# Attention in one transformer layer: two key tiles of values and the due sum in one visit to the 32-column matmuls, sums inverted in transposed blocks

## The chip, the core and the metric

The program runs on one core of a Trainium2 chip. A core has a matrix engine (TensorE; PE in the profile, its weight loads PEld), three elementwise engines (VectorE, DVE; ScalarE, ACT; GpSimd, POOL), and SyncE (SP), which here only issues DMAs. They run at the same time and wait for each other by semaphores. TensorE writes to PSUM, eight banks of 2 KB in each of 128 partitions; POOL does not touch PSUM in this program. The metric is the device time of one execution, in microseconds (us); lower is better.

## The reference

A layer with block-sparse causal self attention, cross attention and a feed-forward block, in 32-bit floats, for B = 4 batch rows, S = 1024 tokens, D = 512 channels, 16 heads of 32 channels. Cut to what matters here:

```python
x = _layernorm(tgt, n1_g, n1_b)
tgt = tgt + _block_sparse_self_attn(x, ...)
x = _layernorm(tgt, n2_g, n2_b)
tgt = tgt + _mha_cross(x, memory, ...)
x = _layernorm(tgt, n3_g, n3_b)
return tgt + jax.nn.relu(x @ ff_w1.T + ff_b1) @ ff_w2.T + ff_b2

# inside each attention
scores = jnp.einsum('bhqd,bhkd->bhqk', q, k) / scale   # self: masked by block and causally
p = jax.nn.softmax(scores, axis=-1)
out = jnp.einsum('bhqk,bhkd->bhqd', p, v)
```

## The kernel before

The layer is a row of stages: projections of the context (tag d_) and of x (a_), self attention (b_), a projection (c_), cross attention (e_), a projection (f_), the feed-forward block (m_). The change touches `attention_stage` alone, which is built twice, with `causal` true for b_ and false for e_.

**A pass.** Four heads of one batch row are worked on together; 4 rows by 4 such head groups make N = 16 passes, numbered n. The 1024 queries are two halves of 512. A pass is a list of steps k, each one tile of 128 keys (t) against one half (h) of queries: 16 steps in cross attention, all 512 queries wide; 12 in self attention, where a tile on the diagonal leaves only the later queries, 384, 256 or 128 columns, and tiles beyond it are left out. `first` is the first query column that a step needs. Each step has four blocks, one for each head j.

**What a step does, and on which engine.**
- TensorE, `scores`: keys by queries into one of two PSUM buffers `st_ps` (tile st). The stationary operand is 128 wide; it also holds rows with the negative row maximum, so that the exponential needs no bias. On the diagonal of self attention a short mask matmul follows (line 1136).
- ScalarE, `exponentials`: exp of a block into `probs`, a ring of PR key tiles (6 in self attention, 8 in cross).
- TensorE, `weigh`: the probabilities against the values of the tile. The stationary operand is 32 columns wide, and the four heads fill four strips of 32 output rows of `pv_ps`. Operands are 32-bit; the profile counts each such matmul twice.
- POOL (line 974): adds the probabilities of the two or three key tiles of a group (`groups`), head by head, in place, onto the first tile of the group.
- TensorE, `sum_up`: a 32-column matrix of ones against the added tile, into `sum_ps`. This gives the softmax sum of each query, the same number on each of the 32 rows of a head. The columns of one group are cut into `parts` (2 or 3), one part at the end of each step.
- ScalarE, `copy_sums` (line 1071): `sum_ps` to `sums`, once each half. VectorE, `copy_outs` (line 988): `pv_ps` to `outs`, once each half.
- VectorE, `normalise`: in pieces of 64 columns (cross) or 128 (self), one piece a step, reciprocal of `sums` and product with `outs`.
- In the same steps TensorE and VectorE prepare the row maxima of the next passes: `max_scores` (tile nat; one or two matmuls for each of 32 units of 128 queries and one head, a unit being t and j) and `maximum` (line 997). In cross attention units alternate between two pairs of PSUM banks, and unit u may be written once unit u-2 is reduced (`reach` is 2; in self attention 2 to 4). Once a pass the 32 columns of maxima are transposed (line 1120) and split in a high and a low part (lines 1006, 1008).

**What sets the order.** Nothing schedules: the loops of `body` on each engine are the order. On TensorE, step k goes over j = 0 to 3 and issues for each j: scores of block (k+1, j); the row-maximum matmuls that the tables `next_units` and `later_units` put there (in cross attention one unit at j = 0 and one at j = 2); after j = 1 `weigh(k)`; after j = 3 the parts of sums due at step k. So values and sums alternate, each between two scores:

```python
if j == 1:
    weigh(n, p, k)
if j == HG - 1:
    for back, g, c in summing[k]:
        if at_least(n, back):
            sum_up(n - back, p - back, g, c)
```

VectorE goes over the same steps and j: copy of outputs at j = 2 of a half's last step, split of maxima, maxima, and at j = 2 the due piece of `normalise`. Passes 1 to 12 run in a loop of three passes an iteration; the others are written out.

**Waits that matter.** `scores` of a block waits for the exponential of two blocks before (`exped`). `sum_up` of a half's first group waits until `sum_ps` is free (`sums_copied`). The exponential into a ring buffer waits for the sum of the tile that lay there (`summed`). The addition of a group waits for the values of its first tile (`weighed`), since it overwrites it.

## Time and profile before

| what | us |
|---|---|
| median of 3 runs | 3573.18 (3571.24 to 3574.4) |
| span of the profiled execution, first to last instruction | 3571.7 |
| self attention, b_ | about 601 to 1349 of the span |
| cross attention, e_ | about 1652 to 2659 |
| feed-forward block, m_ | about 2760 to the end |

The profiled execution's own time was not taken apart from its span, which lies 1.5 us below the median.

How to read the rows below. A row of the view in order of time has the start in us, the time in us, the engine, the line in the kernel, the operation, written and read tiles with their shapes, and the count of like instructions merged in the row. Matmuls are pipelined, so the start of the next row tells more than the time in a row: "start to start" is what an instruction costs its engine. In brackets stands how long the engine (or its weight loader) had been idle before, and what ended the wait. A row of the view by tile has least, median and greatest time of one instruction in ns. e_sum matmuls are the sums, e_pv the values, e_st the scores, e_nat the row maxima.

### The profile page before, as it was taken

The numbers are of one execution on the slowest core, as the hardware profiler recorded it, in microseconds if no ns is written. First come the engines' busy times: TensorE is split into PE (matmuls) and PEld (weight loads), VectorE is DVE, ScalarE is ACT, GpSimd is POOL, SyncE is SP. The second block draws the span as 40 slices with busy tenths as digits, with TensorE's granted clock in tenths as the row PEclk, the third lists the DMA queues.
The fourth block names the chain that finished last, engine by engine and source line by source line (L and its number), as shares of the span: only waits on it lengthen the run. The fifth ranks groups of instructions, "written<-read, shape, count | busy, mean of one in ns | idle before, by whom it ended". The sixth has DMA issues, their size and how long they took to land. (4 is left out here: it accounts for less than half of the span.)

```text
span 3571.7 us, 54829 instructions
## 1 busy us (share of the span) xinstructions
PE 3303.2 (92%) x18570; PEld 2078.1 (58%) x18570; DVE 2124.1 (59%) x2949; ACT 1323.5 (37%) x2369; POOL 1826.2 (51%) x1552
## 2 busy tenths in 40 slices
PE   7969997999999996969999999999968499999999
PEld 6857884545454545754444444444427388888887
DVE  4435545777777765757998989899948611111110
ACT  2112221545455552223665656566642221111111
POOL 3124332444444455644887878788876362222222
PEclk9979996999999998987999999999989799999999
DMA  5535446343444405534332423324026631111110
GB/s 195 177 118 195 170 162 152 83 89 79 88 96 96 96 14 179 214 131 104 73 69 52 93 49 72 74 52 93 10 77 233 250 95 48 51 49 51 50 48 24
DMA packets 211665, 361.36 MB, mean 101 GB/s; under 512 B 16312, under 2 KB 92600, under 8 KB 207312
## 3 DMA queue, kind: packets, MB, share of 16 engines
q1 hardware_dynamic: 211408, 358.01, 35.2%
q8 instruction: 152, 2.49, 0.3%
q14 instruction: 105, 0.86, 0.1%
HBM read 214.20 MB, written 142.61 MB: 100 GB/s over the span
## 5 line engine op out<-in xcount | busy, mean ns | idle before, releaser
L974 POOL TENSOR_TENSOR e_probs<-e_probs 128x512 f32<-128x512 f32 x640 | 799.2, 1280 | 234.6 <-ACT e_probs L1064 228.8
L1064 ACT ACTIVATE e_probs<-e_st 128x512 f32<-128x512 f32 x1024 | 603.4, 597 | 428.5 <-PE e_st L1132 369.6
L997 DVE TENSOR_REDUCE e_neg_max<-e_nat 128x1 f32<-128x1024 f32 x512 | 615.1, 1214 | 92.9 <-PE e_nat L1110 67.1
L974 POOL TENSOR_TENSOR b_probs<-b_probs 128x128 f32<-128x128 f32 (+2 forms) x384 | 341.7, 920 | 427.7 <-ACT b_probs L1064 427.7
L1064 ACT ACTIVATE b_probs<-b_st 128x512 f32<-128x512 f32 (+3 forms) x768 | 367.2, 491 | 419.1 <-PE b_st L1136 331.2
L997 DVE TENSOR_REDUCE b_neg_max<-b_nat 128x1 f32<-128x128 f32 (+7 forms) x512 | 369.5, 751 | 184.0 <-PE b_nat L1114 180.1
L1132 PE MATMUL e_st<-e_qs,e_ks 99*128 99x512 f32 x1024 | 464.0, 459 | 10.4 <-issue 7.6
L1363 DVE CAST m_hid_hi<-m_hid 128x512 fp32r<-128x512 f32 x128 | 59.1, 462 | 599.1 <-ACT m_hid L1315 599.1
L1342 POOL TENSOR_TENSOR m_hid_lo<-m_hid,m_hid_hi 128x512 fp32r<-128x512 f32 x128 | 165.1, 1290 | 461.5 <-DVE m_hid_hi L1363 461.5
L1132 PEld LDWEIGHTS e_st<-e_qs,e_ks 99*128 99x128 f32 x1024 | 192.9, 190 | 339.4 <-ACT e_probs L1064 233.2
L1110 PE MATMUL e_nat<-e_ks,e_qs 96*128 96x512 f32 x1024 | 351.6, 429 | 27.0 <-DVE e_neg_max L997 15.5
L1132 PE MATMUL b_st<-b_qs,b_ks 99*128 99x512 f32 (+2 forms) x768 | 332.2, 447 | 10.0 <-issue 9.0
L1315 ACT ACTIVATE m_hid<-m_h_ps,m_b 128x512 f32<-128x512 f32 x128 | 88.2, 689 | 589.8 <-PE m_h_ps L117 589.8
L1147 PE MATMUL e_pv<-e_probs,e_vs 128*32 128x512 f32 x2048 | 278.0, 615 | 0.5 <-ACT e_probs L1064 0.5
L1110 PE MATMUL b_nat<-b_ks,b_qs 97*128 97x384 f32 (+4 forms) x768 | 249.3, 410 | 26.3 <-DMA b_ks<-b_key_mask 19.3
L1132 PEld LDWEIGHTS b_st<-b_qs,b_ks 99*128 99x128 f32 x768 | 150.6, 196 | 202.2 <-ACT b_probs L1064 149.8
L1110 PEld LDWEIGHTS e_nat<-e_ks,e_qs 96*128 96x128 f32 x1024 | 199.5, 202 | 81.1 <-DVE e_neg_max L997 42.5
L117 PE MATMUL m_h_ps<-m_x_hi,m_w_hi 128*128 128x512 f32 x512 | 201.4, 393 | 24.0 <-DMA m_x_lo<-xt_lo 21.7
L117 PE MATMUL m_o_ps<-m_w_hi,m_hid_hi 128*128 128x512 f32 x512 | 202.6, 396 | 0.6 <-POOL m_hid_lo L1342 0.6
L117 PE MATMUL m_o_ps<-m_w_lo,m_hid_hi 128*128 128x512 f32 x512 | 202.5, 396 | 0.0
L117 PE MATMUL m_o_ps<-m_w_hi,m_hid_lo 128*128 128x512 f32 x512 | 202.4, 395 | 0.0
L117 PE MATMUL m_h_ps<-m_x_lo,m_w_hi 128*128 128x512 f32 x512 | 201.7, 394 | 0.0
(195 smaller groups left out, 5815.2 us busy)
## 6 DMA issues: line engine op xcount, KB each, us to landing
b_qs<-sq_hi SPq DMA_DIRECT2D x30, 512.0 KB, 7.4
b_ks<-sk_hi SPq DMA_DIRECT2D x30, 512.0 KB, 14.3
e_qs<-cq_hi SPq DMA_DIRECT2D x30, 512.0 KB, 6.6
e_ks<-ck_hi SPq DMA_DIRECT2D x30, 512.0 KB, 14.5
d_x<-in_ctx SPq DMA_DIRECT2D x8, 1024.0 KB, 6.3
ck_hi<-d_part_hi SPq DMA_DIRECT2D x32, 256.0 KB, 5.7
ck_lo<-d_part_lo SPq DMA_DIRECT2D x32, 256.0 KB, 5.9
cv<-d_tok_out SPq DMA_DIRECT2D x32, 256.0 KB, 5.4
```

The costliest lines, as they stand in the source:

```text
L117: last = pe.matmul(out, w, x, start=(start and n == 0 and m == 0), stop=(stop and n == len(pairs) - 1 and m == 2))
L974: last = pool.tensor_tensor(here, here, there, ALU.add)
L997: dve.tensor_reduce(neg_max[:, u:u + 1], nat[:, bank_of[u]:bank_of[u] + banks, 0:keys // banks], AX.XY, ALU.max, negate=True).then_inc(max ...
L1064: act.activation(probs[:, (p * NS + k) % PR, j, first:TOK], st_ps[:, blk % 2, first:TOK], ACT.Exp).then_inc(exped, 1)
L1110: last = pe.matmul(nat[:, bank_of[u] + bank, 0:cols], qs[p][0:rows, j, t * P:(t + 1) * P], ks[p][0:rows, j, bank * width:bank * width + co ...
L1132: last = pe.matmul(st_ps[:, blk % 2, lo:TOK], ks[p][0:ROWS, j, t * P:(t + 1) * P], qs[p][0:ROWS, j, h * TOK + lo:(h + 1) * TOK], start=Tru ...
L1147: last = pe.matmul(pv_ps[j * DH:(j + 1) * DH, first:TOK], vs[p][:, t, j * DH:(j + 1) * DH], probs[:, (p * NS + k) % PR, j, first:TOK], sta ...
L1315: act.activation(hid[:, c % RING, :], h_ps[:, c % RING, :], ACT.Relu, bias=b1_sb[:, c:c + 1]).then_inc(relu_done, 1)
L1342: pool.tensor_tensor(hid_lo[:, c % RING, :], hid[:, c % RING, :], hid_hi[:, c % RING, :].bitcast(F32), ALU.subtract).then_inc(hid_lo_done, 1)
L1363: dve.tensor_copy(hid_hi[:, c % RING, :], hid[:, c % RING, :]).then_inc(hid_hi_done, 1)
```

## The change

- **Windows.** `weigh` of two key tiles is done in one place, after j = 1 of the odd steps, for steps k-1 and k, and the sum that is due at k follows at once. The values of even tiles so come one step later. A sum is no longer cut in parts: one call does all columns of its group. `groups` now gives, for each group, its first step, its length and the (odd) step at which its sum is due: in cross attention 5, 9, 11 in the first half and 13, 17, 19 in the second, in self attention first step + 5; numbers beyond the pass fall into the next one.
- **Ring.** PR is 9 in self attention (6 before), 8 in cross as before.
- **Additions.** POOL adds four heads in one instruction.
- **Inversion.** `copy_sums` on ScalarE and the tile `sums` go. Instead VectorE transposes `sum_ps` in blocks of 32x32 to `turned_sums`; in it each block holds 32 different sums down its rows and the same number along its columns, so one column of each of the 16 blocks (128x16) is inverted; a second blockwise transpose of that, each column repeated 32 times, writes the inverses back to `sum_ps`. In the step after, one product of 128x512 of `outs` and `sum_ps` normalises the half. A half's inversion stands behind the maxima of j = 2: in cross attention at steps 11 and 19 (3 of the next pass), in self attention at 7 and 15 (3 of the next); the product one step later. `sum_ps` is free for the next half after the product.
- SP stores each half after one count of `normalised`; the first half's store of a pass stands behind the row loads of the next pass in both stages.

```diff
-    PR = 6 if causal else 8
+    PR = 9 if causal else 8
...
     if causal:
-        groups = [(k, 2, 2, k + 3) for k in range(0, NS, 2)]
+        groups = [(k, 2, k + 5) for k in range(0, NS, 2)]
     else:
-        assert KT == 8
-        groups = [(h * KT + k, *g) for h in range(HALVES) for k, g in
-                  ((0, (3, 3, h * KT + 4)), (3, (3, 3, h * KT + 7)), (6, (2, 2, h * KT + 10)))]
+        groups = [(h * KT + k, length, h * KT + at) for h in range(HALVES) for k, length, at in
+                  ((0, 3, 5), (3, 3, 9), (6, 2, 11))]
...
+    invert_steps = [groups[group_of[last_step[h]]][2] for h in range(HALVES)]
+    normal_steps = [at + 1 for at in invert_steps]
...
-                            for j in range(HG):
-                                here, there = (probs[:, (p * NS + i) % PR, j, first:TOK] for i in (k, k + more))
-                                last = pool.tensor_tensor(here, here, there, ALU.add)
-                            last.then_inc(added, 1)
+                            pool.tensor_tensor(here, here, there, ALU.add).then_inc(added, 1)
...
-                def normalise(n, h, c):
...
-                    dve.reciprocal(sums[:, h, cols], sums[:, h, cols]).then_inc(inverted, 1)
-                    dve.wait_ge(inverted, done + 1)
-                    dve.tensor_tensor(outs[:, h, cols], outs[:, h, cols], sums[:, h, cols],
-                                      ALU.mult).then_inc(normalised, 1)
+                def invert(n, h):
...
+                    dve.wait_ge(summed, n * NSUM + group_of[last_step[h]] + 1)
+                    dve.transpose(turned_sums[:], sum_ps[:]).then_inc(sums_turned, 1)
+                    dve.wait_ge(sums_turned, n * HALVES + h + 1)
+                    dve.reciprocal(inverse[:], turned_sums[:].rearrange("p (b i) -> p b i", i=32)[:, :, 0]).then_inc(inverted, 1)
+                    dve.wait_ge(inverted, n * HALVES + h + 1)
+                    dve.transpose(sum_ps[:], inverse[:].unsqueeze(2).to_broadcast([P, TOK // 32, 32])).then_inc(spread, 1)
+
+                def normalise(n, h):
+                    dve.wait_ge(spread, n * HALVES + h + 1)
+                    dve.wait_ge(outs_copied, n * HALVES + h + 1)
+                    dve.tensor_tensor(outs[:, h, :], outs[:, h, :], sum_ps[:], ALU.mult).then_inc(normalised, 1)
...
-                    act.copy(sums[:, h, :], sum_ps[:]).then_inc(sums_copied, 1)
...
+                def sum_up(n, p, g):
+
+                    k, length, _ = groups[g]
+                    h, t, first = steps[k]
+                    pe.wait_ge(added, n * ADDITIONS + additions(g + 1))
+                    if t == 0 and (h or at_least(n, 1)):
+                        pe.wait_ge(normalised, n * HALVES + h)
                     for j in range(HG):
...
+                        last = pe.matmul(sum_ps[j * DH:(j + 1) * DH, first:TOK], ones[:],
+                                         probs[:, (p * NS + k) % PR, j, first:TOK], start=(t == 0),
+                                         stop=(k + length - 1 == last_step[h]), skip_group_check=True)
                     last.then_inc(summed, 1)
+
+                def window(n, p, k):
+                    weigh(n, p, k - 1)
+                    weigh(n, p, k)
+                    for back, g in due[k]:
+                        if at_least(n, back):
+                            sum_up(n - back, p - back, g)
...
-                            if j == 1:
-                                weigh(n, p, k)
-                            if j == HG - 1:
-                                for back, g, c in summing[k]:
-                                    if at_least(n, back):
-                                        sum_up(n - back, p - back, g, c)
+                            if j == 1 and k % 2:
+                                window(n, p, k)
```

TensorE before, cross attention, first pass, two steps: scores (e_st), row maxima (e_nat), values (e_pv) and a part of sums (e_sum) in turn.

```order
L1147 MATMUL e_pv<-e_probs,e_vs 32x512 x4
L1132 MATMUL e_st<-e_qs,e_ks 128x512
L1110 MATMUL e_nat<-e_ks,e_qs 128x512 x2
L1132 MATMUL e_st<-e_qs,e_ks 128x512
L1164 MATMUL e_sum<-e_probs,e_ones 32x171 x4
L1132 MATMUL e_st<-e_qs,e_ks 128x512
L1110 MATMUL e_nat<-e_ks,e_qs 128x512 x2
L1132 MATMUL e_st<-e_qs,e_ks 128x512
L1147 MATMUL e_pv<-e_probs,e_vs 32x512 x4
```

The same engine and pass after the change, from one window to the next, two steps later.

```order
L1100 MATMUL e_st<-e_qs,e_ks 128x512
L1078 MATMUL e_nat<-e_ks,e_qs 128x512 x2
L1100 MATMUL e_st<-e_qs,e_ks 128x512 x2
L1078 MATMUL e_nat<-e_ks,e_qs 128x512 x2
L1100 MATMUL e_st<-e_qs,e_ks 128x512 x2
L1078 MATMUL e_nat<-e_ks,e_qs 128x512 x2
L1100 MATMUL e_st<-e_qs,e_ks 128x512 x2
L1078 MATMUL e_nat<-e_ks,e_qs 128x512 x2
L1100 MATMUL e_st<-e_qs,e_ks 128x512
L1115 MATMUL e_pv<-e_probs,e_vs 32x512 x8
L1128 MATMUL e_sum<-e_probs,e_ones 32x512 x4
```

Where every second scores matmul had a visit beside it, eight scores and four pairs of row-maximum matmuls now follow each other, and eight value matmuls and the four of the sum stand together.

VectorE before, cross attention, first pass, from the copy of the first half's outputs on: pieces of 64 columns between the row maxima.

```order
L988 COPY e_outs<-e_pv 128x512
L997 TENSOR_REDUCE e_neg_max<-e_nat 128x1 x11
L1017 RECIPROCAL e_sums<-e_sums 128x64
L1019 TENSOR_TENSOR e_outs<-e_outs,e_sums 128x64
L997 TENSOR_REDUCE e_neg_max<-e_nat 128x1
L1006 CAST e_max_hi<-e_nat 32x128
```

The same after the change.

```order
L965 COPY e_outs<-e_pv 128x512
L974 TENSOR_REDUCE e_neg_max<-e_nat 128x1 x9
L991 STREAM_TRANSPOSE e_turned_sums<-e_sum 128x512
L993 RECIPROCAL e_inverse<-e_turned_sums 128x16
L995 STREAM_TRANSPOSE e_sum<-e_inverse 128x512
L974 TENSOR_REDUCE e_neg_max<-e_nat 128x1 x2
L1000 TENSOR_TENSOR e_outs<-e_outs,e_sum 128x512
L974 TENSOR_REDUCE e_neg_max<-e_nat 128x1
L983 CAST e_max_hi<-e_nat 32x128
```

The inversion is three instructions in a row behind nine maxima (the last of them that of step 11, j = 2), the product stands two maxima later, and the pieces of 64 columns are gone from the following steps.

## Rows read from the trace of the kernel before

**Rows 1.** Busy us (and instructions) by stage: window, length, PE, PEld, DVE, ACT, POOL; clock, DMA, GB/s.

```profile
610.00:1340.00 730.00, 714.03 (x5479) 360.56 (x5475) 536.28 (x779) 376.17 (x791) 339.72 (x380) 0.98 0.37 80
1660.00:2640.00 980.00, 958.47 (x6004) 417.62 (x6000) 850.46 (x1018) 612.51 (x1045) 789.32 (x632) 0.98 0.27 60
```

**Rows 2.** Order of time, PE, cross attention in full swing: start, us, engine, what.

```profile
2114.18 0.64 PE L1164 MATMUL e_sum<-e_probs,e_ones 128*32 128x256 f32 x8
2114.75 0.50 PE L1132 MATMUL e_st<-e_qs,e_ks 99*128 99x512 f32 x1
2115.09 0.64 PE L1110 MATMUL e_nat<-e_ks,e_qs 96*128 96x512 f32 x2
2115.56 0.40 PE L1132 MATMUL e_st<-e_qs,e_ks 99*128 99x512 f32 x1
2115.89 1.07 PE L1147 MATMUL e_pv<-e_probs,e_vs 128*32 128x512 f32 x8
2116.89 0.51 PE L1132 MATMUL e_st<-e_qs,e_ks 99*128 99x512 f32 x1
```

**Rows 3.** Order of time, DVE: copies of outputs of the same half, one pass apart.

```profile
1775.30 0.67 DVE L988 COPY e_outs<-e_pv 128x512 f32<-128x512 f32 x1
...
1835.82 0.68 DVE L988 COPY e_outs<-e_pv 128x512 f32<-128x512 f32 x1
```

**Rows 4.** Order of time, first pass of cross attention, a step without sums.

```profile
1666.58 0.50 PE L1132 MATMUL e_st<-e_qs,e_ks 99*128 99x512 f32 x1
...
1667.12 2.49 ACT L1064 ACTIVATE e_probs<-e_st 128x512 f32<-128x512 f32 x4 [0.83 <-PE e_st L1132]
...
1667.77 0.19 PEld L1132 LDWEIGHTS e_st<-e_qs,e_ks 99*128 99x128 f32 x1 [0.42 <-ACT e_probs L1064]
...
1668.58 0.40 PE L1132 MATMUL e_st<-e_qs,e_ks 99*128 99x512 f32 x1
```

**Rows 5.** By tile: exponentials and POOL's additions of one head, cross attention.

```profile
L1064 ACT ACTIVATE e_probs<-e_st x1024: 591/597/632, 1653.1 to 2642.6; 128x512 f32<-128x512 f32 x171
L974 POOL TENSOR_TENSOR e_probs<-e_probs x640: 1258/1280/1307, 1661.9 to 2648.8; 128x512 f32<-128x512 f32 x160
```

**Rows 6.** Order of time, PE, last pass of cross attention: three thirds of a sum together.

```profile
2645.20 1.08 PE L1164 MATMUL e_sum<-e_probs,e_ones 128*32 128x170 f32 x24 [0.91 <-POOL e_probs L974]
```

**Rows 7.** VectorE's operations: two rows in order of time, then by tile (ns least/median/greatest).

```profile
1663.60 0.63 PE L1110 MATMUL e_nat<-e_ks,e_qs 96*128 96x512 f32 x2
...
1664.27 2.40 DVE L997 TENSOR_REDUCE e_neg_max<-e_nat 128x1 f32<-128x1024 f32 x2 [0.91 <-PE e_nat L1110]
...
1777.88 3.47 DVE L997 TENSOR_REDUCE e_neg_max<-e_nat 128x1 f32<-128x1024 f32 x3
...
L988 DVE COPY e_outs<-e_pv x32: 673/674/692, 1684.1 to 2644.4; 128x512 f32<-128x512 f32 x32
...
L1017 DVE RECIPROCAL b_sums<-b_sums x128: 929/943/952, 637.5 to 1347.8; 128x128 f32<-128x128 f32 x128
...
L1019 DVE TENSOR_TENSOR e_outs<-e_outs,e_sums x256: 224/640/1300, 1705.5 to 2658.4; 128x64 f32<-128x64 f32 x128
...
L1008 DVE TENSOR_TENSOR e_max_lo<-e_nat,e_max_hi x16: 278/278/279, 1646.9 to 2590.1; 32x128 fp32r<-32x128 f32 x16
```

**Rows 8.** Self attention: the same sum visit one pass apart, and exponentials by tile.

```profile
743.84 0.64 PE L1164 MATMUL b_sum<-b_probs,b_ones 128*32 128x256 f32 x8
...
789.69 0.64 PE L1164 MATMUL b_sum<-b_probs,b_ones 128*32 128x256 f32 x8
...
L1064 ACT ACTIVATE b_probs<-b_st x768: 272/542/632, 602.8 to 1340.8; 128x512 f32<-128x512 f32 x96, 128x384 f32<-128x384 f32 x32, 128x256 f32<-128x256 f32 x32, 128x128 f32<-128x128 f32 x32
```

**Rows 9.** Order of time, DVE, last pass of cross attention: both copies of outputs, last product.

```profile
2619.98 0.69 DVE L988 COPY e_outs<-e_pv 128x512 f32<-128x512 f32 x1 [6.22 <-PE e_pv L1147]
...
2644.36 0.69 DVE L988 COPY e_outs<-e_pv 128x512 f32<-128x512 f32 x1 [7.94 <-PE e_pv L1147]
...
2658.35 0.23 DVE L1019 TENSOR_TENSOR e_outs<-e_outs,e_sums 128x64 f32<-128x64 f32 x1
```

More of the change, by code:

```diff
@@ L962, in body @@
                 def body(n, m, p):
[L963 removed]
+                    for g, (k, length, _) in enumerate(groups):
                         for more in range(1, length):
[L965 removed]
                             first = steps[k + more][2]
+                            here, there = (probs[:, (p * NS + i) % PR, :, first:TOK] for i in (k, k + more))
                             pool.wait_ge(exped, n * NBLOCKS + (k + more + 1) * HG)
```

97 lines of the change are left out of this document (25 added, 72 removed).

## Prediction

> **What bounds the kernel now.** I read the table by stage first, then the order of time of each engine inside one attention step. Two stretches hold the edited code: self attention (b_) and cross attention (e_). TensorE is busy 714 of 730 us in the first and 958 of 980 in the second, at a granted clock of 0.98; POOL has 789 of 980 and VectorE 850 of 980 in the second [rows 1]. So TensorE's own order sets the time, and anything else counts only where it makes TensorE wait.
>
> Inside a cross attention step (key tile k, four heads) a half-step is: scores (e_st), two row-maximum matmuls (e_nat), scores, and then a visit to the 32-column matmuls, once with values (e_pv), once with sums (e_sum). In [rows 2] the reader sees a sum visit of 256 columns last 0.57 us (start to next start) and a value visit of 512 columns 1.00. Hence 0.43 us per 256 columns of four heads and 0.14 fixed per visit. The scores after a visit take 0.34, those before one 0.33, where a maximum matmul in mid-stream takes 0.235 (0.47 for two). A removed visit could so give 0.14 + 0.10 + 0.10 = 0.34 us. A half-step is 0.34 + 0.47 + 0.33 = 1.14; two of them with visits of 1.00 and 0.43 to 0.57 make 3.71 to 3.85 a step, and 16 steps 60.0. A pass (one batch row and head group; 16 in each stage) takes 60.52 from output copy to output copy [rows 3]; TensorE is the bound with 0.5 to spare.
>
> In [rows 4] stand steps of the first pass, where no sums are due, so that two half-steps follow each other with no visit between. That is the pattern which the change makes everywhere. There scores(j=0) start 1.19 us after scores(j=2), not 2 x 0.34 + 0.47 = 1.05 or less, and their weight load waits for ScalarE. There are two score buffers: scores start, the exponential starts 0.54 later, takes 0.60 [rows 5], and its buffer is free 0.05 after its end: 1.19 for two heads, however free TensorE is. With a visit between half-steps (1.14 + 0.43) this round trip is hidden today.
>
> **The change part by part.**
>
> *Visits.* Cross attention goes from 32 visits a pass to 8 (windows), self attention from 24 to 6. One visit with more of the same costs only the streaming: the 24 sum matmuls of [rows 6] (three thirds of 512 columns in one go) take 1.08 against 1.07 for one value visit [rows 2]. So a window with two value tiles is 1.00 + 0.86 = 1.86, and with a sum of 512 columns 2.72. Streaming does not change: each sum had the same columns in parts.
>
> *Cross attention, what lies between windows.* Four half-steps: 3 x 1.19 by the round trip, then 0.81 to the last scores [rows 4] and 0.33 to the window [rows 2]: 4.71. Six windows have a sum, two have none: 8 x 4.71 + 6 x 2.72 + 2 x 1.86 = 57.7 us a pass. Against 60.5 that is 2.8 less, where 24 visits at 0.34 promised 8.2: the round trip takes back two thirds.
>
> *Inversion on VectorE.* Removed in each pass: 16 reciprocals of 64 columns and 16 products of 64 columns (mean wait on POOL included, 0.64 each), and two copies of sums on ScalarE. Added for each half: transpose 128x512, reciprocal 128x16, transpose 128x512, product 128x512. No row shows a VectorE transpose. Nearest is the copy PSUM to SBUF of the same size, 0.67 [rows 7]; I take 0.70. Below: hardly under 0.6, as it moves 512 columns. Above: twice the copy, 1.35. The reciprocal is 0.94 for 128 columns [rows 7], and 0.24 taken for 16 (between 0.12, its share, and 0.5). With 0.04 between dependent instructions the inversion is 0.70 + 0.24 + 0.70 + 0.10 = 1.75. The Trainium skill, "VectorE: DVE Perf Modes", section "The three transpose paths", gives 311 ns for 128x128 in bf16; with 384 more columns at the copy's pace that would be about 0.7 too, and the sum would stay.
>
> The total of VectorE falls, but this 1.75 is in one piece, at step 11 (and 3), behind the maximum of j=2 and ahead of that of the next step. Queued behind it are the maxima; for them waits TensorE's second maximum matmul pair after it, as a bank pair is reused every second unit. Walked from a window's end at 0: first maximum matmuls 0.34, reduce 0.67 later [rows 7] from 1.01 to 2.21; inversion 2.14 to 3.85; next reduce to 5.0. TensorE wants to write that bank pair at 3.57 + 0.34 = 3.9 and starts at 5.1; with its weight load then open, 1.3 us lost. Nothing hides it: before a window VectorE runs at 1.13 per reduce (3.47 for three [rows 7], so (3.47 - 1.21) / 2) against one each 1.19. The next window hides the product (0.7), which ends near 6.8, ahead of the sum that waits for it at 7.8. Two such losses a pass, 2.6, and 0.2 more where the turned maxima meet the denser maxima. Cross attention: 57.7 + 2.6 + 0.2 = 60.5 against 60.5. No gain.
>
> *Self attention.* 45.85 us a pass [rows 8] in 24 visits and 24 half-steps. Visits: 7168 columns at 0.43 per 256 = 12.0, and 24 x 0.14 = 3.4; so the half-steps hold 30.4. After it 12.0 + 6 x 0.14 = 12.9 of windows. Each half-step must now be at least 1.19 (512 wide) down to 0.86 (128 wide, as the exponential is 0.27 there [rows 8]). Taken one by one, the ones with few maxima (four right after windows, and the narrow ones) rise to their floor and the heavy ones lose 0.2: 30.1 (26.8 if no floor held, 18 x 0.2 less; 30.4 if all did), so 43.0. The inversion at step 7 holds back the 1024-wide maximum, 1.3; at step 3 it falls where no maxima are queued, nothing. Denser maxima elsewhere: at step 4 the one of 1024 columns is read until 0.4 after its bank is wanted, and smaller ones of 0.3 in sum: 0.7. So 45.0, a gain of 0.85 a pass.
>
> *POOL.* Four heads in one addition: 128x512 took 1.28 [rows 5], so at most 5.1, perhaps 4.6 for one start. It starts a step later for even tiles, since the value matmul it must follow moved; its sum is also due later. Worst case, three tiles: ready 10 us after the window at step 1, due 14 after it. Ten a pass are 51 of 60 us. Costs nothing; it would from 6 us an addition on. ScalarE reuses a probabilities buffer after its sum: sum matmuls stand ahead of the scores concerned on TensorE by half a step at least (with nine buffers in self attention, eight in cross), so that wait stays empty.
>
> *Ends.* In the last pass, which has no maxima, 8 steps are 24.4 us [rows 9], 3.05 each; a pair of steps becomes 3 x 1.19 + 0.85 + 2.72 = 7.14 against 6.1: 6 us lost in cross, 3 in self attention. After the last values the old end took 14.2 us (copy at 2644.36 to product at 2658.35 + 0.23 [rows 9]); now POOL's last addition (4.2 after the values), sums 1.0, inversion and product 2.7: 8. That gives back 6, and 3 in self attention. SP's loads wait for the last value matmul of a pass, which stays at the last step; its stores wait for one count a half where it was 4 or 8, and the row loads they are moved behind come first anyway.
>
> **Sum.** 14 passes x 0.85 = 12 in self attention, 0 in cross, ends -1: 11 us off. The profiled execution spans 3571.7 us, 1.5 below the median 3573.2; the same difference from the median gives 3562.
>
> **The rivals.**
>
> *The inversion is hidden* (0.15). If VectorE gets through it in the slack of windows, 3 losses x 16 passes x 1.3 = 62 us stay away: 3500. For: VectorE's sum falls by a quarter. Against: the walk above, bank by bank.
>
> *Each removed switch pays in full* (0.06). (24 + 18) x 16 x 0.34 = 229 us, less 62 for the inversion: 3405. For: the 0.34 of [rows 2]. Against: the 1.19 of [rows 4]. The Trainium skill, "TensorEngine Tiling (Array Packing)", section "Key Properties", says that a change of tiling mode drains the array; the 0.33 and 0.14 of [rows 2] agree, but the Trainium skill says nothing there of what a drain hides, here the exponentials.
>
> *Slower: the transposes are slow* (0.22). At 1.35 each the inversion is 3.05, and every 1 us of it costs 48 us (three places, 16 passes): +62, 3624. It decides from 0.38 us more than taken, transposes of 0.9, where the kernel passes 3580. For: no row has one. Against: the copy's 0.67.
>
> *Slower: the product waits for POOL* (0.04). Products of two SBUF operands took 0.22 to 1.30, ending with POOL's instruction, which now lasts 5 us [rows 7]. Mean wait 2.5, slack 1.1: 1.4 x 64 = 90, 3650. Against: the new product reads PSUM, and the subtraction with PSUM and SBUF operands took 278 to 279 ns however POOL stood [rows 7]. The Trainium skill, "SBUF — State Buffer", section "SBUF: two separate sides", names only two SBUF inputs or a 2-port mode as taking the lock; the trace agrees.
>
> *Gains and losses cancel* (0.08): 3573.
>
> **How the numbers follow.** The forecast has 0.45, its own range 3535 to 3588, as half a microsecond off in a pass of either stage is 8 us. Within 0.2% (3566 to 3580) is about what a measurement can tell from no change. Faster by more: 0.27 of the forecast, 0.15 and 0.06, 0.48. Same: 0.12 of the forecast and 0.08, 0.20. Slower: 0.06 of the forecast, 0.22 and 0.04, 0.32. The range for 8 in 10 leaves out the full gain and the POOL rival and the ends: 3495 to 3625.
>
> **What would show it.** Windows of 1.86 and 2.72 us; scores 1.19 apart between them with the weight load waiting on ScalarE (right), or under 1.0 (wrong). TensorE's maximum matmuls idle 1.2 us, released by a reduce, right after each inversion in cross attention. Passes of 60.5 and 45.0 us. Transposes of 0.7; product 0.7 and steady; additions of 4.6 to 5.1. It is wrong if the back edges of the loops cost other than now, or if the inversion's loss is not where I place it.

## Result: slower by 2.2%, and the profile after

The changed kernel takes 3651.3 us (median of 4, 3637.4 to 3663.5) against 3573.8 for the kernel before on the same chip: ratio 1.022, 95% interval 1.019 to 1.024. The profiled execution took 3652.5 and spans 3649.4, 77.7 more than before. The prediction said 3562, with a range that ended at 3625: wrong in sign, and outside.

From its first to its last copy of outputs self attention takes 41.7 us more, cross attention 45.4. Below is the table by stage of the changed kernel (columns as in [rows 1]). TensorE's busy time fell a little in both windows, but it now idles 65 and 74 us in them (16 and 22 in [rows 1]), and its granted clock fell from 0.98 to 0.95 and 0.96.

```profile
610.00:1382.00 772.00, 707.37 (x4721) 369.07 (x4724) 431.12 (x656) 350.69 (x759) 297.23 (x95) 0.95 0.34 76
1700.00:2722.00 1022.00, 948.24 (x4735) 418.16 (x4734) 653.67 (x656) 569.37 (x1010) 724.53 (x159) 0.96 0.26 57
```

First the parts, since most came out as forecast. By tile (least, median, greatest in ns): the transposes take 0.706 and 0.727 us, the reciprocal 0.253, the product 0.671 (at most 0.687, however POOL stands), an addition of four heads 4.57.

```profile
L991 DVE STREAM_TRANSPOSE e_turned_sums<-e_sum x32: 705/706/718, 1737.4 to 2731.6; 128x512 f32<-128x512 f32 x32
L993 DVE RECIPROCAL e_inverse<-e_turned_sums x32: 253/253/255, 1738.1 to 2732.4; 128x16 f32<-128x16 f32 x32
L995 DVE STREAM_TRANSPOSE e_sum<-e_inverse x32: 726/727/728, 1738.4 to 2732.7; 128x512 f32<-128x512 f32 x32
L1000 DVE TENSOR_TENSOR e_outs<-e_outs,e_sum x32: 671/671/687, 1741.3 to 2733.4; 128x512 f32<-128x512 f32 x32
L952 POOL TENSOR_TENSOR e_probs<-e_probs x160: 4517/4567/4600, 1699.2 to 2725.5; 128x2048 f32<-128x2048 f32 x160
```

Order of time on TensorE, a window of cross attention with its sum (2.71 us, 1992.75 to 1995.46) and what follows it. The scores matmuls start 1.19 apart in pairs, and the last row is the wait that the inversion causes.

```profile
1992.75 1.92 PE L1115 MATMUL e_pv<-e_probs,e_vs 128*32 128x512 f32 x16
1994.49 1.04 PE L1128 MATMUL e_sum<-e_probs,e_ones 128*32 128x512 f32 x8
1995.46 0.50 PE L1100 MATMUL e_st<-e_qs,e_ks 99*128 99x512 f32 x1
1995.80 0.63 PE L1078 MATMUL e_nat<-e_ks,e_qs 96*128 96x512 f32 x2
1996.27 0.88 PE L1100 MATMUL e_st<-e_qs,e_ks 99*128 99x512 f32 x2
...
1997.46 0.88 PE L1100 MATMUL e_st<-e_qs,e_ks 99*128 99x512 f32 x2
...
1998.65 0.88 PE L1100 MATMUL e_st<-e_qs,e_ks 99*128 99x512 f32 x2
2000.51 0.74 PE L1078 MATMUL e_nat<-e_ks,e_qs 96*128 96x512 f32 x2 [0.97 <-DVE e_neg_max L974]
```

VectorE at the same place. The reduce of step 11 runs first, then the inversion, then the reduce for which TensorE waits. The prediction put the inversion at 2.14 to 3.85 us after the window's end; measured are 2.15 to 3.90.

```profile
1996.47 1.23 DVE L974 TENSOR_REDUCE e_neg_max<-e_nat 128x1 f32<-128x1024 f32 x1 [2.62 <-PE e_nat L1078]
1997.61 0.71 DVE L991 STREAM_TRANSPOSE e_turned_sums<-e_sum 128x512 f32<-128x512 f32 x1
1998.35 0.25 DVE L993 RECIPROCAL e_inverse<-e_turned_sums 128x16 f32<-128x16 f32 x1
1998.63 0.73 DVE L995 STREAM_TRANSPOSE e_sum<-e_inverse 128x512 f32<-128x512 f32 x1
1999.27 2.32 DVE L974 TENSOR_REDUCE e_neg_max<-e_nat 128x1 f32<-128x1024 f32 x2
```

From one window start to the next, a pair of steps with nothing else in it takes 7.43 us with a sum and 6.56 without; one with an inversion takes 8.66. A cross pass has, from window to window beginning at step 1: 7.50, 8.66, 7.43, 6.56, 7.50, 8.66, then 8.85 to 9.59, and 7.42 to 8.29. The last two are those that the prediction did not foresee. First, from step 13 to 15:

```profile
2067.80 0.27 PE L1088 MATMUL e_nat<-ident,e_neg_max 128*32 128x128 f32 x1
2067.95 0.50 PE L1100 MATMUL e_st<-e_qs,e_ks 99*128 99x512 f32 x1
2068.76 0.73 PE L1078 MATMUL e_nat<-e_ks,e_qs 96*128 96x512 f32 x2 [0.31 <-DVE e_max_lo L985]
...
2071.68 0.75 PE L1100 MATMUL e_st<-e_qs,e_ks 99*128 99x512 f32 x1 [0.77 <-DMA e_qs<-e_max_lo]
2072.22 1.05 PE L1078 MATMUL e_nat<-e_ks,e_qs 96*128 96x512 f32 x2
2073.08 0.63 PE L1100 MATMUL e_st<-e_qs,e_ks 99*128 99x512 f32 x1
2073.64 2.65 PE L1115 MATMUL e_pv<-e_probs,e_vs 128*32 128x512 f32 x16
2076.22 0.51 PE L1100 MATMUL e_st<-e_qs,e_ks 99*128 99x512 f32 x1
```

TensorE transposes the row maxima (L1088), VectorE splits them (first wait, 0.31 us), SyncE sends them into the rows of `qs`, and the scores of the next pass, issued one step ahead at step 15, wait for them: here 0.77 us. The second of the two DMAs lands at 2071.55, 3.75 us after the transpose, and the scores start 0.13 later. One pass earlier the scores again start 0.13 behind the landing, though the profile names ScalarE there. After the wait shown the value matmuls of a window take 2.58 (2073.64 to 2076.22) where others take 1.85; in that earlier pass, with waits of 0.42 and 0.76, they take 1.85 at a clock of 1.00. So the waits alone do not tell whether the clock falls. Second, from step 15 to step 1, five units of maxima lie between two windows where there are four elsewhere. On TensorE four e_nat matmuls stand in a row (two units in one slot), and on VectorE five reduces, 5.81 us, in a stretch that elsewhere takes 4.71:

```profile
2013.72 1.49 PE L1078 MATMUL e_nat<-e_ks,e_qs 96*128 96x512 f32 x4
...
2013.20 5.81 DVE L974 TENSOR_REDUCE e_neg_max<-e_nat 128x1 f32<-128x1024 f32 x5 [0.17 <-PE e_nat L1078]
```

The copies of outputs give the account by stage. First and last of the 32 in cross attention:

```profile
1720.51 0.69 DVE L965 COPY e_outs<-e_pv 128x512 f32<-128x512 f32 x1 [0.90 <-PE e_pv L1115]
...
2726.23 0.69 DVE L965 COPY e_outs<-e_pv 128x512 f32<-128x512 f32 x1 [11.54 <-PE e_pv L1115]
```

Worked out from all 32 of each stage (mean pass without back edges, times 14; what the three back edges of the loop add; the last three halves; the rest of the program):

| us, after minus before | forecast | measured |
|---|---|---|
| self attention, 14 passes | -12 (45.0 each) | +22.5 (47.46 each) |
| cross attention, 14 passes | 0 (60.5 each) | +44.2 (63.7 each) |
| back edges, self and cross | 0 | +5.8 and -14.0 |
| last passes, and what follows them | +1 | +28.7 and -9.4 |
| sum | -11 | +77.8 |

### The profile page after: what moved, and what is told of

It reads as the page before. It is cut to its first block and busy times, and to the rows that moved or that the text cites. A ratio compares the mean times of both kernels' runs of the same rounds, so it can differ in the third digit from the quotient of the medians.

```text
span 3649.4 us, 49032 instructions
## 1 busy us (share of the span) xinstructions
PE 3292.3 (90%) x16522; PEld 2090.6 (57%) x16522; DVE 1815.9 (50%) x2437; ACT 1257.7 (34%) x2305; POOL 1714.6 (47%) x784
## 5 line engine op out<-in xcount | busy, mean ns | idle before, releaser
L952 POOL TENSOR_TENSOR e_probs<-e_probs 128x2048 f32<-128x2048 f32 x160 | 730.8, 4568 | 345.7 <-PE e_pv L1115 285.1
L1042 ACT ACTIVATE e_probs<-e_st 128x512 f32<-128x512 f32 x1024 | 577.7, 596 | 515.7 <-PE e_st L1100 457.0
L952 POOL TENSOR_TENSOR b_probs<-b_probs 128x1536 f32<-128x1536 f32 (+1 forms) x96 | 298.5, 3109 | 512.9 <-PE b_pv L1115 401.5
L1042 ACT ACTIVATE b_probs<-b_st 128x512 f32<-128x512 f32 (+3 forms) x768 | 355.7, 490 | 488.3 <-PE b_st L1104 371.1
L1329 DVE CAST m_hid_hi<-m_hid 128x512 fp32r<-128x512 f32 x128 | 59.6, 466 | 597.4 <-ACT m_hid L1281 597.4
L1100 PE MATMUL b_st<-b_qs,b_ks 99*128 99x512 f32 (+2 forms) x768 | 314.3, 445 | 41.9 <-ACT b_probs L1042 24.8
L1115 PE MATMUL e_pv<-e_probs,e_vs 128*32 128x512 f32 x2048 | 266.6, 642 | 0.0
```

The lines of the kernel that those rows point to most:

```text
L952: pool.tensor_tensor(here, here, there, ALU.add).then_inc(added, 1)
L1042: act.activation(probs[:, (p * NS + k) % PR, j, first:TOK], st_ps[:, blk % 2, first:TOK], ACT.Exp).then_inc(exped, 1)
L1100: last = pe.matmul(st_ps[:, blk % 2, lo:TOK], ks[p][0:ROWS, j, t * P:(t + 1) * P], qs[p][0:ROWS, j, h * TOK + lo:(h + 1) * TOK], start=Tru ...
L1115: last = pe.matmul(pv_ps[j * DH:(j + 1) * DH, first:TOK], vs[p][:, t, j * DH:(j + 1) * DH], probs[:, (p * NS + k) % PR, j, first:TOK], sta ...
L1329: dve.tensor_copy(hid_hi[:, c % RING, :], hid[:, c % RING, :]).then_inc(hid_hi_done, 1)
```

## Experiments

Each has the kernel before beside it on the same chip (medians 3571 to 3573 us). "Pass" below is the time from copy to copy of outputs in the middle of a stage, away from back edges.

**1. Inversion first.** VectorE does the inversion ahead of the maxima of j = 2.

```diff
+                            if j == HG // 2:
+                                for half in range(HALVES):
+                                    if invert_steps[half] % NS == k and at_least(n, invert_steps[half] // NS):
+                                        invert(n - invert_steps[half] // NS, half)
                             if k == TURN and j == TURN_HEAD and not is_last(n):
                                 split_max(nn[0], (n, m, p))
```

> The changed kernel with one move on VectorE: the inversion (transpose, reciprocal, transpose) stands ahead of the maxima of step 11 (3) and not behind the first of them; products as they were. Theory (place): TensorE idles 0.97 to 1.03 at maximum matmuls after each inversion in cross attention and once a pass in self attention, because the inversion delays a reduce that TensorE needs 3.9 us after the window; put first, it runs in the 1.0 us in which VectorE has no maxima yet, delays the next reduce by 0.7 only, and that one is not needed before 3.6. So pairs of 8.66 us become 7.43: 32 x 1.2 = 39 us in cross, 16 x 1.0 = 16 in self attention, and up to 16 more where the clock stays up after it: 3651 - 55 to 71 = 3580 to 3596. Rival (load): VectorE has one reduce of 1.21 each 1.19 us between windows and no slack anywhere, so 1.7 us of inversion cost the same wherever they stand: within 10 us of 3651.

Measured: 3597.4 us, ratio to before 1.006 (1.004 to 1.009). Order of time on VectorE after the window at step 11: the transpose starts when the sum ends.

```profile
1838.54 0.72 DVE L991 STREAM_TRANSPOSE e_turned_sums<-e_sum 128x512 f32<-128x512 f32 x1 [1.76 <-PE e_sum L1131]
...
1840.21 3.45 DVE L974 TENSOR_REDUCE e_neg_max<-e_nat 128x1 f32<-128x1024 f32 x3
```

On TensorE, in the same place, the wait of 0.97 has become 0.16:

```profile
1841.45 0.73 PE L1081 MATMUL e_nat<-e_ks,e_qs 96*128 96x512 f32 x2 [0.16 <-DVE e_neg_max L974]
```

Pairs of 8.66 became 7.84, a cross pass 60.85, a self attention pass 45.8. The place theory holds, with 0.4 us of each loss left and a time 1 us above its range; the load theory falls.

**2. Maxima turned one step earlier.**

```diff
-    LAG = 3
+    LAG = 4
```

> The changed kernel with the transpose of the row maxima one step earlier (step 12 in cross, 8 in self attention), so that a window lies between it and the scores of the next pass, which need its rows back from a DMA. Theory (round trip): since the change only 3 to 4 us of TensorE work lie between the two, the way split, DMA, landing takes 3.5 to 4.5, so that TensorE idles 0.75 a pass and in every second pass runs its next window at the half clock. Earlier, this wait hides under a window: pair from step 13 to 15 8.85 to 9.59 becomes 7.43 to 7.8, 16 x 1.4 to 1.9 = 22 to 30 us in cross attention, up to 8 in self attention: 3615 to 3630. The 0.3 to 0.4 us wait for the split part stays. Rival: the stall there is VectorE's, late by its own work, and the rows would have come in time: within 5 us of 3651.

Measured: 3633.6 us, 1.016 (1.013 to 1.019), 4 us slower than the range of the round-trip theory. The wait for the rows is gone, but a new one stands at the transpose, which needs all maxima while VectorE is held up by the inversion one step before; and the window after it runs at the half clock (value matmuls 3.42 us):

```profile
1862.60 0.28 PE L1088 MATMUL e_nat<-ident,e_neg_max 128*32 128x128 f32 x1 [1.47 <-DVE e_neg_max L974]
...
1865.15 3.64 PE L1115 MATMUL e_pv<-e_probs,e_vs 128*32 128x512 f32 x16
1868.57 1.77 PE L1128 MATMUL e_sum<-e_probs,e_ones 128*32 128x512 f32 x8
```

**3. Filler.** In the last pass, which has no maxima, matmuls of no use in TensorE's gaps.

```diff
+                            if is_last(n) and k < NS - 1 and j in (0, 2):
...
+                                for bank in range(2):
+                                    pe.matmul(nat[:, bank, :], qs[p][0:AUG, j, 0:P],
+                                              ks[p][0:AUG, j, 0:512], start=True, stop=True)
```

> The changed kernel with more work for TensorE: in the last pass of both stages, which has no row maxima, two 96x512 matmuls of no use after the scores of j = 0 and 2 (28 or more in each stage), in the gaps in which TensorE waits for exponentials. Theory (clock): the last pass took 92.7 us in cross and 75.8 in self attention from copy to copy against 77.4 and 62.4 before, 15.3 and 13.4 more, and only about half of that is the round trip of the exponentials; the rest is windows at the half clock (value matmuls of two tiles 2.87 to 3.14 instead of 1.74). Filled gaps keep the clock up: all windows at 1.74 and 2.71, last passes shorter by 5 to 7 us in each stage in spite of more matmuls: 3637 to 3641. Rival (the clock has another cause than idle gaps): the same windows at half clock, time the same or longer by some us.

Measured: 3645.6 us (3631.0 to 3652.1), 1.021 (1.020 to 1.023), above the range that was expected: by the median it can't be told from the changed kernel. The traces can. The last cross pass took 86.9 us from copy to copy (92.7 without filler), the last of self attention 72.5 (75.8). By stretches of the changed kernel, two windows and the whole pass (the number after the five busy times is the clock):

```profile
2670.20:2673.00 2.80, 2.80 (x17) 0.69 (x20) 0.00 (x0) 0.68 (x2) 0.71 (x1) 0.59 0.00 0
2678.50:2680.20 1.70, 1.70 (x17) 0.53 (x20) 0.00 (x0) 0.69 (x2) 1.70 (x1) 1.00 0.05 10
...
2659.70:2726.00 66.30, 58.75 (x261) 18.53 (x264) 6.15 (x10) 36.01 (x66) 46.05 (x11) 0.87 0.03 13
```

The same pass with filler:

```profile
2644.10:2708.30 64.20, 62.23 (x332) 27.56 (x331) 8.65 (x15) 38.89 (x70) 50.56 (x12) 1.00 0.04 14
```

The value matmuls of two windows, equal work, take 2.87 and 1.74 us, at clocks of 0.59 and 1.00 (the half clock for most of it, 1.2 of 2.4 GHz, and the full one). In the pass with filler every window is at the full clock, and the pass is shorter although TensorE does more. So in the last passes a part of what the waits for exponentials cost is the clock that falls behind them. No run filled the gaps of the other passes.

**4. One part alone: additions of four heads in the kernel before.**

```diff
-                            for j in range(HG):
-                                here, there = (probs[:, (p * NS + i) % PR, j, first:TOK] for i in (k, k + more))
-                                last = pool.tensor_tensor(here, here, there, ALU.add)
-                            last.then_inc(added, 1)
+                            here, there = (probs[:, (p * NS + i) % PR, :, first:TOK] for i in (k, k + more))
+                            pool.tensor_tensor(here, here, there, ALU.add).then_inc(added, 1)
```

> The kernel before with one part of the change alone: POOL adds four heads in one instruction (4.57 us instead of four of 1.28). Prediction on record: it costs nothing in the changed kernel, as POOL is not late. Here the old products of VectorE read two SBUF operands and end with POOL's instruction. Theory (lock): each of 16 products a pass in cross attention now waits up to 4.6 us, 1.8 on average instead of 0.4; VectorE goes from 850 to some 1150 of 980 us and becomes the bound: 3700 to 3900. Rival (POOL's form does not matter to VectorE): products keep their median of 0.64, time 3565 to 3580.

Measured: 4227 us, 1.186 (1.181 to 1.192), worse than the theory. By tile, the old product of 64 columns went from a median of 0.64 [rows 7] to 1.84, at most 4.26:

```profile
L1017 DVE TENSOR_TENSOR e_outs<-e_outs,e_sums x256: 224/1841/4256, 1924.6 to 3312.2; 128x64 f32<-128x64 f32 x128
```

In order of time, one such product on VectorE:

```profile
2399.03 3.92 DVE L1017 TENSOR_TENSOR e_outs<-e_outs,e_sums 128x64 f32<-128x64 f32 x1
```

And the addition on POOL in the midst of which it starts, and with which it ends, at 2402.9:

```profile
2398.30 4.56 POOL L973 TENSOR_TENSOR e_probs<-e_probs 128x2048 f32<-128x2048 f32 x1 [7.04 <-ACT e_probs L1062]
```

TensorE waits for none of POOL's additions in this cross attention; behind VectorE's reduces it stands 255 us, and its clock in a stretch of that stage is 0.82 (0.98 in [rows 1]), which the theory had left out:

```profile
PE e_nat L1108 <- DVE e_neg_max L995: 254.9, 103, 6.6
...
2000.00:3000.00 1000.00, 794.87 (x4115) 327.96 (x4114) 868.41 (x726) 415.96 (x706) 484.98 (x108) 0.82 0.22 47
```

So the long addition costs nothing beside a product with an operand in PSUM (0.671 in the changed kernel), but much beside one of two SBUF operands. The Trainium skill, "SBUF — State Buffer", section "SBUF: two separate sides", says as much of two SBUF inputs; the trace agrees: the product of 3.92 us ends with the addition.

**5. Both moves, 1 and 2.** The diffs of both; the second is:

```diff
-    LAG = 3
+    LAG = 4
```

> Both moves at once: inversion ahead of the maxima and the transpose of the row maxima one step earlier. Alone the second brought 18 us and not 22 to 30 because a new wait came in: TensorE's transpose at step 12 needs all maxima, and VectorE, held up by the inversion at step 11, was 1.47 us late. Theory: with the inversion out of the way that wait goes too, so that the pair of steps from 11 to 13 takes 7.4 to 7.9 and the one from 13 to 15 also; a cross pass 59.2 to 59.6 instead of 60.85 (inversion first) and 63.4 (change): 3597 - 21 to 26, less up to 8 in self attention: 3565 to 3576. Rival (the late maxima are late by their number, not by the inversion): at least 0.7 us of the wait stays and the clock falls after it as before: 3585 to 3600.

Measured: 3593.5 us, 1.006 (1.005 to 1.008), in the rival's range, though not for its reason. A cross pass takes 60.45: the wait of 1.47 is gone (0.16 is left), but the stretch with five units stands as before, now between steps 13 and 15 (5.57 between windows). In self attention the passes of one and the same program take 44.5 us or 47.6, whole iterations of the loop at a time: with about the same waits, the stretch after the window of step 7 takes 7.2 us at a clock of 1.00, or 8.7 at about 0.8, with a next window of 3.8 to 4.2 us and not 2.5. That is the clock again. The 44.5 lies below the 45.85 of the kernel before: where the clock stays up, the windows do gain in self attention.

**6. No inversion** (left out; the product multiplies by the sums).

```diff
-                    dve.transpose(turned_sums[:], sum_ps[:]).then_inc(sums_turned, 1)
...
-                    dve.reciprocal(inverse[:], turned_sums[:].rearrange("p (b i) -> p b i", i=32)[:, :, 0]).then_inc(inverted, 1)
...
-                    dve.transpose(sum_ps[:], inverse[:].unsqueeze(2).to_broadcast([P, TOK // 32, 32])).then_inc(spread, 1)
```

> The changed kernel with the inversion left out (both transposes and the reciprocal; the product multiplies by the sums themselves, so what it puts out is not the attention). It prices the inversion as a whole, wherever it costs. By the term of the prediction (1.3 us lost at two places a pass in cross attention, one in self attention, none at step 3 of self attention): pairs of 8.66 become 7.43, self attention's gap after step 7 6.74 becomes 5.7, the one after step 3 stays 5.81; cross pass 60.1 to 61.6, self attention 45.4 to 47: 3651 - 39 - 16 = 3596, down to 3575 where the clock then stays up. Rival (inversion also costs at step 3 of self attention and at the turn): the gap of 5.81 shrinks to 5.0 to 5.5 and the time is below 3575.

Measured: 3575.5 us, 1.000 (0.999 to 1.002). Cross passes 60.05 (62.5 with inversion and clock up): 2.5 for two inversions, forecast 2.6. Self attention 45.3 against 46.4: 1.1, forecast 1.3. The gap after step 3 stays 5.81, so an inversion there costs nothing, as forecast; what fills it is in the trace: a wait of 0.45 for the exponential where a half-step has no maxima, and a maximum matmul that comes 0.33 late behind a reduce further on. The inversion so costs 14 x 3.6 = 50 us of the 76 that the time fell; the other 26 lie in passes at the half clock, in the last passes and at back edges, and were not taken apart. The row of the 0.45:

```profile
755.11 0.73 PE L1095 MATMUL b_st<-b_qs,b_ks 99*128 99x512 f32 x2
756.29 0.50 PE L1095 MATMUL b_st<-b_qs,b_ks 99*128 99x512 f32 x1 [0.45 <-ACT b_probs L1037]
```

**7. As 5, with one unit of maxima in each slot of cross attention.**

```diff
-        place.append(START + at - NBLOCKS)
+        place.append(START + (at if causal else 2 * u) - NBLOCKS)
```

> The changed kernel with inversion first, maxima turned one step earlier, and, in cross attention, the 32 row-maximum units laid one in each of the 32 slots; the table puts two (units 5 and 6) at step 0, j = 0 (with the earlier turn at step 15, j = 0) and none at one slot five steps on. Theory: the stretch after the window ahead of that slot has five reduces of 1.21 in the place of four, which is why it takes 5.56 and not 4.71; with one unit a slot it takes 4.71, a cross pass 60.45 - 0.86 = 59.6, 3594 - 14 = 3580. Rival (it is the backlog from the copy of outputs or from the split of maxima): it stays 5.5, 3594 within 5.

Measured: 3581.5 us, 1.002 (1.000 to 1.003). The stretch takes 4.72 and not 5.57, a cross pass 59.6, as expected. In the table of the kernel before the same two units lie in one slot; there a visit stands on either side, and the stretch between them takes 1.93 us where others take 1.14, 0.79 more with 0.47 of it the matmuls' own; the empty slot later gives 0.38 back. With its windows mended in three places, the change is about level with the kernel before. Its self attention still takes 47.6 us in most passes.

**8. One visit a step** (with inversion first).

```diff
-                    weigh(n, p, k - 1)
                     weigh(n, p, k)
...
-                            if j == 1 and k % 2:
+                            if j == 1:
```

> Inversion first, and in place of a window every second step one visit at each step: the values of that tile and the sum that is due, 16 visits a pass in cross attention (windows 8, before 32), 12 in self attention (6, 24). Theory (round trip): two half-steps between visits cost 1.19 + 0.81 + 0.33 = 2.33 (2.28 with a visit between them), so nearly as little as before, where four in a row cost 4.71; and a visit of 1.00 every 2.33 lets VectorE catch up, so that inversion and transposed maxima cost nothing. Cross pass: 16 x 2.33 + 16 x 1.00 + 6 x 0.86 + 0.5 = 59.0; self attention 45.85 less 12 x 0.14 to 12 x 0.34: 41.8 to 44.1. 3571 - 24 - 28 to 65: 3482 to 3519, clock at 0.98 in both stages. Rival (what the change pays for is the inversion and the additions, not the length of the stretch between windows): stalls of TensorE on maxima stay, 3560 to 3600.

Measured: 3554.8 us, 0.995 (0.994 to 0.997): faster, but 36 above the range. Cross attention is near (59.8, stretches of 2.33 and visits of 1.00 and 1.86 to the hundredth, the slot with two units 3.19). Self attention is not: 46.5, where 41.8 to 44.1 was said. Against experiment 1, which differs in the windows alone, the kernel is 43 us faster.

**9. Visits apart.** Values at j = 1 of each step, the due sum after j = 3, the inversion ahead of the next maximum.

```diff
-                            if j == 1 and k % 2:
-                                window(n, p, k)
+                            if j == 1:
+                                weigh(n, p, k)
+                            if j == HG - 1:
+                                for back, g in due[k]:
+                                    if at_least(n, back):
+                                        sum_up(n - back, p - back, g)
```

> The changed kernel with the visits taken apart again: values of each step after j = 1, the due sum (all columns, one call) after j = 3 of its step, the inversion ahead of the next maximum; additions and inversion as changed. 22 visits a pass in cross attention, 18 in self attention. It prices the change without its windows. Theory (windows cost, the rest gains): cross pass 16 x 1.00 + 6 x 1.00 + 6 x 2.28 + 10 x 2.33 + 0.5 = 59.5, self attention 45.85 - 6 x 0.14 = 45.0: 3571 - 16 - 14 = 3541, in any case below 3560. Rival (the inversion costs wherever it is): above 3571.

Measured: 3538.7 us, 0.990 (0.987 to 0.993). Cross pass 59.33, self attention 46.15. So of all that was changed it is the windows that lose: with the new inversion and additions, and visits apart, the kernel is 113 us faster than with windows. Of these, experiment 1 had 54 with the windows kept, by the place of the inversion alone; 59 are left between the two versions in which the inversion costs little.

**10. Mixed.** Self attention as in the kernel before; cross attention as 9, one unit a slot as in 7.

```diff
-        attention_stage(nc, "b_", ident, *(by_group(qk[n]) for n in ("sq_hi", "sq_lo", "sk_hi", "sk_lo")),
+        attention_stage_as_before(nc, "b_", ident, *(by_group(qk[n]) for n in ("sq_hi", "sq_lo", "sk_hi", "sk_lo")),
```

> Self attention wholly as in the kernel before; cross attention with visits apart (values each step, the due sum in one call after j = 3), the inversion ahead of the next maximum, one unit of maxima a slot. Theory: self attention's visits are narrow and stand between heavy half-steps already, so none of the change gains there: 721.8 us from first to last copy as before, against 740.0 with visits apart. Cross pass 59.33 less up to 0.4 for the slot with two units: 58.9 to 59.3. 3538.7 - 18 + 3 - 0 to 7 = 3516 to 3524. Rival (self attention's 18 us come back elsewhere, by clock or back edges): 3530 to 3540.

Measured: 3524.4 us, 0.986 (0.984 to 0.988), the fastest version here, 49 us below the kernel before. By stage (cross attention, columns as above) TensorE idles 16 of 942 us at a clock of 0.99.

```profile
1655.00:2597.00 942.00, 926.45 (x4770) 389.21 (x4773) 667.45 (x659) 590.35 (x1016) 728.70 (x160) 0.99 0.28 62
```

**11. Whole sums.** The kernel before, with this and with one unit a slot in cross attention.

```diff
-                  ((0, (3, 3, h * KT + 4)), (3, (3, 3, h * KT + 7)), (6, (2, 2, h * KT + 10)))]
+                  ((0, (3, 1, h * KT + 5)), (3, (3, 1, h * KT + 9)), (6, (2, 1, h * KT + 11)))]
```

> The kernel before with two edits in cross attention alone: each sum in one call at the step where the change has it due (3 visits a half in the place of 8), and one unit of maxima a slot. Sums copied by ScalarE, pieces of 64 columns on VectorE, additions of one head, self attention: all as before. It tells what of the 49 us that the mixed version gains comes from fewer visits, and what from the new inversion and the additions. Theory (visits): inversion and additions never stood in TensorE's way, so a cross pass is the mixed version's 58.9 to 59.3, 3524 to 3532. Rival (the pieces on VectorE delay maxima where two half-steps follow each other): TensorE idles at maxima behind the pieces, pass 59.8 to 60.5, 3540 to 3570.

Measured: 3556.4 us, 0.996 (0.994 to 0.998). The time lies in the rival's range, but its idling is not there: TensorE waits 13 us in all behind reduces, 16 in the kernel before. A cross pass takes 59.46, between the two ranges (60.57 before, 58.92 mixed): two thirds of what a pass gains come from fewer visits and even slots, which were not tried apart. What else the mixed version has lies at the back edges, which add 32 us to three passes here and 16 there, and 9 after the last copy. By its waits, VectorE stands 8.6 us at each of three back edges with nothing that the profile shows it waiting for, here as in the kernel before; with the new inversion there is no such row. The row has the sum in us, the count and the longest:

```profile
DVE e_neg_max L997 <- issue: 25.6, 3, 8.6
```

## Where the prediction was right, and which steps failed

- **Windows, round trip, walk of the inversion: right.** Measured and, in brackets, forecast: windows 2.71 and 1.86 us (2.72 and 1.86), between them 4.71 to 4.79 (4.71), the inversion 1.23 a place in cross attention and 1.1 in self attention (1.3), product steady, POOL hidden. The full gain from removed switches and the slow transposes are refuted by these rows, POOL's lock by the steady 0.671; the inversion is not hidden where it stands, and nearly is one place earlier (experiment 1), which the prediction did not try.
- **"Cross attention: 57.7 + 2.6 + 0.2 = 60.5": one term mis-sized, one missing.** The 0.2 was for the turned maxima, and that pair costs 1.4 more. The step on SP said that the row loads "come first anyway"; it looked at their order on the queue and not at who waits for them. Before, a sum visit of step 13 and both visits of step 14 lay between the transpose and the scores that need the rows, which came 4.5 us after it (rows of the kernel before, below); the change moved the visits away, and without a wait the scores would come after 3.0. By the starts in the trace about 0.55 of the 1.4 is the wait for the split and 0.87 the wait for the rows. In experiment 7 the pair from 13 to 15 is down to 7.43, so the wait for rows is gone; but the pair of the turn, which now also holds an inversion, takes 8.77 where one with an inversion alone took 7.84 (experiment 1), with waits of 0.40 for the split and twice 0.17 for reduces. So the earlier turn moved most of the cost and saved only 0.4 a pass. The missing term is the double slot, 0.86 (experiment 7): the kernel's description gave cross attention one unit at j = 0 and one at j = 2, but the table puts two at step 0, j = 0, and none at a slot five steps on. 60.5 + 1.2 + 0.9 = 62.6 against 62.5 where the clock stays up.

```profile
1767.92 0.27 PE L1120 MATMUL e_nat<-ident,e_neg_max 128*32 128x128 f32 x1
1768.13 0.50 PE L1164 MATMUL e_sum<-e_probs,e_ones 128*32 128x171 f32 x8
...
1769.89 1.06 PE L1147 MATMUL e_pv<-e_probs,e_vs 128*32 128x512 f32 x8
...
1772.02 0.50 PE L1164 MATMUL e_sum<-e_probs,e_ones 128*32 128x171 f32 x8
1772.45 0.50 PE L1132 MATMUL e_st<-e_qs,e_ks 99*128 99x512 f32 x1
```

- **The clock was not in the sum.** Nothing in the prediction asked what TensorE's new waits do to its clock, though it stood in the table of [rows 1] at 0.98. In more than half of the passes a window behind such waits runs partly at the half clock, about 1.5 us more: 1.2 a pass on average in cross attention (63.7 less 62.5), 1.1 in self attention (47.5 less 46.4). The last passes were forecast 9 us longer, for the round trip alone, and are 28.7 longer; experiment 3 brings 9 of the 20 that were not foreseen back by filler, and the rest was not taken apart. That the clock falls because of the waits is shown for the last passes alone.
- **"Self attention 43.0": mis-sized by 1.6.** Without inversion and with the clock up it is 45.3 (experiment 6), where 43.0 + 0.7 was said. 18 removed visits were to save 0.2 each at heavy half-steps, but half-steps without maxima wait 0.45 at the floor and clumps of four units wait for VectorE in the middle of a stretch; the six stretches hold 32.4 us, not less than the 30.5 of before but more. For 24, 18, 12 and 6 visits a pass took 45.85 (before), 46.15 (experiment 9), 46.5 (8) and 45.8 (1, clock up): joining visits gained next to nothing. With the turn one step earlier six visits took 44.5 in the iterations where the clock stays up (experiment 5), so most of the 1.6 hangs on where the turn and its maxima stand; what part is whose stays open.
- **Back edges.** Named as a risk, not priced: 5.8 lost in self attention, 14.0 won in cross attention, where VectorE's stand of 8.6 us goes.

Together: passes 67 us instead of -12, last passes and ends 19 instead of +1, edges -8: the 89 us between 3562 and 3651. Of the 79 in the passes about 32 are the clock (14 x 1.2 and 14 x 1.1), 28 cross attention's two terms and 20 self attention's half-steps (rounded, worked out from the passes with the clock up).

## What to carry to other kernels

Joining visits saves a fixed cost only as long as the stretch between them stays full. Here the rows priced a visit at 0.34 us, but ten fewer of them in each cross pass gave 1.1 us (experiment 11), and visits were also the cover for the round trip of exponentials, for VectorE's backlog and for a DMA that comes back a step later. Before moving work, list for each wait how much work lies between the request and its use, before and after; a dependent chain through another engine's queue counts as much as one through data. When a matrix engine begins to wait, price the clock too. And try the parts of a change alone: one (long additions) can be ruinous without the other (a product that reads PSUM), and one (windows) can hide what the rest gains.

## What the runs showed of the hardware

- Behind short waits TensorE's clock sometimes falls for the work that follows: in the last pass of cross attention a stretch of value matmuls took 2.87 us at a clock of 0.59 where the same work took 1.74 at 1.00. The same waits (0.3 to 0.8 us) come with and without the fall from pass to pass, and the state can last: passes of the same loop body took 44.5 or 47.6 us for a whole iteration. Matmuls of no use in the gaps of the last pass kept the clock at 1.00.
- A VectorE product of 64 columns with both operands in SBUF can last 4.26 us when POOL runs an instruction of 4.5 us; one of 128x512 with an operand in PSUM takes 0.67 at any time beside it.
- A blockwise transpose of 128x512 on VectorE takes 0.71 us from PSUM to SBUF and 0.73 back, near the 0.67 of a copy.
- A stand of 8.6 us on VectorE at a loop's back edge is gone in the versions with the new inversion, where VectorE has fewer instructions (1018 before and 656 after in the windows by stage of cross attention). The cause was not taken apart.
